# A four-layer graph network on one core: how the input tiles of the four projections are turned

## What is computed

```python
# layer 0: masked attention with 8 heads of 64
keys, queries, values = x @ Wks, x @ Wqs, x @ Wvs
x = layernorm(x + softmax(queries @ keys.T / 8 - 1e16 * (1 - adj)) @ values @ Wo)
# layer 1
x = layernorm(x + relu((adj @ x) @ W1.T + b1))
# layer 2
h, support = x @ edge_w, x @ weight
att = softmax(x @ node_w, axis=0) * softmax(where(adj > 0, h @ h.T, NEG_BIG), axis=1)
x = layernorm(x + (adj * att) @ support + b2)
# layer 3
x = layernorm(x + relu((a_norm @ x) @ W3.T + b3))      # a_norm: adj + I, scaled by degrees
```

## Time and profile before

| | us |
|---|---|
| median of 3 runs | 2541.1 (2539.39 to 2542.22) |
| profiled execution, its own time | 2541.41 |
| its span from first to last instruction | 2539.6 |
| PE busy | 2424.1, 95% of the span |
| DVE, ACT, POOL busy | 1545.9, 1364.0, 1148.7 |

### The profile page before, as it was taken

The page is one execution under the profiler, slowest core; times in us unless marked ns, Lnnn a source line. Parts: engine busy times, 40 slices in busy tenths (PEclk is TensorE's granted clock), DMA queues, the critical chain, the costliest instruction groups (busy, mean ns, idle before and its releaser), DMA issues. The chain is left out here.

```text
span 2539.6 us, 67049 instructions
## 1 busy us (share of the span) xinstructions
PE 2424.1 (95%) x24988; PEld 1557.7 (61%) x24988; DVE 1545.9 (61%) x3013; ACT 1364.0 (54%) x2036; POOL 1148.7 (45%) x971
## 2 busy tenths in 40 slices
PE   7997999999999999999879997999999999979998
PEld 6885777777777777777634443774444555534443
DVE  4435998898888898888632222555555566633222
ACT  3335888888888888888623221324434444323222
POOL 0005888888888888888601232001111113310323
PEclk9998999999999999999989999999999999989999
DMA  3216999999999999999743654215666779733664
GB/s 130 65 62 129 183 195 185 188 193 181 190 193 178 187 193 184 191 188 185 123 137 118 213 199 158 100 37 138 175 183 181 203 207 233 178 128 101 211 213 140
DMA packets 783644, 417.41 MB, mean 164 GB/s; under 512 B 691296, under 2 KB 717664, under 8 KB 774496
## 3 DMA queue, kind: packets, MB, share of 16 engines
q1 hardware_dynamic: 783456, 414.62, 70.7%
HBM read 203.55 MB, written 40.84 MB: 96 GB/s over the span
## 5 line engine op out<-in xcount | busy, mean ns | idle before, releaser
L806 DVE CUSTOM_DVE_ANT_0 att_scores<-att_slots,att_adj 128x1024 f32<-128x1024 f32 x528 | 575.7, 1091 | 41.6 <-POOL att_part_low L627 14.5
L627 POOL TENSOR_TENSOR att_part_low<-att_scores,att_part_high 128x1024 f16<-128x1024 f32 x352 | 574.8, 1651 | 12.0 <-ACT att_part_high L790 1.1
L751 ACT ACTIVATE att_scores<-att_scores,att_nmax 128x1024 f32<-128x1024 f32 x528 | 552.4, 1047 | 28.2 <-DVE att_lifted L817 26.0
L672 PE MATMUL att_slots<-l_kk,att_q 128*128 128x512 f16 x2112 | 466.5, 356 | 15.5 <-DMA att_q<-q_rows 8.9
L1345 PE MATMUL a_ps<-l_y,a_adj 128*128 128x512 f16 x1936 | 421.2, 381 | 9.0 <-DVE a_adj L1359 4.7
L825 DVE TENSOR_TENSOR att_near_low<-att_ps_t,att_near_high 128x512 f16<-128x512 f32 x528 | 316.4, 599 | 37.6 <-ACT att_near_high L760 35.9
L760 ACT ACTIVATE att_near_high<-att_ps_t 128x512 f16<-128x512 f32 x528 | 258.2, 524 | 150.0 <-PE att_ps_t L682 137.3
L1345 PEld LDWEIGHTS a_ps<-l_y,a_adj 128*128 128x128 f16 x1936 | 190.0, 98 | 240.1 <-DVE a_adj L1359 5.2
L672 PEld LDWEIGHTS att_slots<-l_kk,att_q 128*128 128x128 f16 x2112 | 195.2, 98 | 173.4 <-DVE att_least L806 24.9
L1090 PE MATMUL edge_ps_o<-l_sup,edge_pt_high 128*128 128x512 f16 x968 | 287.9, 379 | 1.7 <-DMA edge_pt_low<-edge_part_low 1.7
L1330 ACT ACTIVATE a_adj<-l_adj 128x2816 f16<-128x2816 f32 x44 | 112.0, 2549 | 291.1 <-DMA l_adj<-in_adj_cols 271.1
(11 more groups left out here) (152 smaller groups left out, 3863.2 us busy)
## 6 DMA issues: line engine op xcount, KB each, us to landing
l_adj<-in_adj_cols SPq DMA_DIRECT2D x44, 1408.0 KB, 6.1
l_adj_tiles<-in_adj SPq DMA_DIRECT2D x22, 1354.0 KB, 6.1
att_adj<-in_adj SPq DMA_DIRECT2D x66, 384.0 KB, 4.2
p_x_in<-x SPq DMA_DIRECT2D x66, 256.0 KB, 2.6
att_q<-q_rows SPq DMA_DIRECT2D x44, 256.0 KB, 3.8
a_xres<-x SPq DMA_DIRECT2D x44, 256.0 KB, 2.8
p_x_in<-in_x SPq DMA_DIRECT2D x22, 256.0 KB, 2.7
q_rows<-l0w_q_halves SPq DMA_DIRECT2D x22, 256.0 KB, 2.1
```

The lines of the kernel that those rows point to most:

```text
L627: nc.gpsimd.tensor_tensor(out=part[1][:, v, lo:lo + width], in0=sc[:, v, lo:lo + width], in1=part[0][:, v, lo:lo + width], op=ALU.subtract ...
L672: mm = nc.tensor.matmul(slots[:, slot, z:z + w], q[:, u, h % 2, a, h // 2, :], kk[:, h, lo + z:lo + z + w], start=a == 0, stop=a == 1)
L751: nc.scalar.activation(sc[:, v, lo:lo + width], sc[:, v, lo:lo + width], ACT.Exp, bias=nmax[:, v:v + 1], scale=-1.0).then_inc(exp_done, 1)
L806: nc.vector.tensor_tensor_reduce(out=sc[:, v, lo:lo + width], in0=slots[:, (NC * h + c) % 2, 0:width], in1=adj[:, u, lo:lo + width], scale ...
```

## The change

- p0 gets its input from the host in column form already (`x_cols`, the same number of bytes per tile, `columns=True`); there is nothing to turn, and the halves are made from `x_in`. Its loops stay as they are.
- p1, p2 and p3 read x in rows as before, but ACT and DVE split the rows first, from `x_in` in SBUF into a new f16 buffer `xr` of two tiles. Then SP issues two transposing transfers for each tile (one for each half, 128 x 512 f16, four blocks of 128 x 128), from `xr` to `xt`, which now holds four tiles. PE waits for both (`turned`, 32 for a tile).
- The PE transposes and their two PSUM banks are gone from all four projections.
- SP's order in p1 to p3: `late` is load(t), then the transposing transfers of tile t - 1. The load of tile 1 moves ahead of all but the first weight.
- In p1 to p3 the loops are written out (`each`).

```diff
-    def load(self, sp):
-        for (src, stage, _h, _l), loaded in zip(self.parts, self.loaded):
+    def load(self, sp, which=slice(None)):
+        for (src, stage, _h, _l), loaded in zip(self.parts[which], self.loaded[which]):
             sp.dma_start(stage, src).then_inc(loaded, 16)
...
+def each(eng, begin, end, step):
+
+
+    for t in range(begin, end):
+        step(t // 2, t % 2)
+
...
-        xt = s.sb("xt", [P, 2, 2, J, P], F16)
+        depth = 2 if columns else 4
+        xt = s.sb("xt", [P, depth, 2, J, P], F16)
+        xr = xt[:, :, :, :, :].rearrange("p u a j r -> p u a (j r)") if columns else s.sb("xr", [P, 2, 2, D], F16)
         junk = s.sb("junk", [P, D])
-        ps_t = s.ps("ps_t", [P, 2, BANK])
         ps_job = [s.ps(f"ps_job{n}", [P, 2, BANK]) for n in range(len(jobs))]
         x_loaded = [s.sem(f"x_loaded{u}") for u in range(2)]
-        turned = s.sem("turned")
         xt_high = s.sem("xt_high")
         xt_low = s.sem("xt_low")
+        turned = [s.sem(f"turned{u}") for u in range(2)]
...
+        over = pairs if columns else each
...
-                    sp.wait_ge(turned, 2 * m + u - 1)
+                    sp.wait_ge(xt_low, 2 * m + u - 1)
                     if score is not None:
                         sp.wait_ge(scored, 2 * m + u - 1)
-                sp.dma_start(x_in[:, u, :], x_rows[bass.ds((2 * m + u) * P, P), :]) \
-                    .then_inc(x_loaded[u], 16)
+                src = x_rows[bass.ds((2 * m + u), 1), :, :].rearrange("o p n -> (o p) n") if columns \
+                    else x_rows[bass.ds((2 * m + u) * P, P), :]
+                sp.dma_start(x_in[:, u, :], src).then_inc(x_loaded[u], 16)
...
+            def turn(m, u):
+
+                if not columns:
+                    t = 2 * m + u
+                    sp.wait_ge(xt_low, t + 1)
+                    if t >= depth:
+                        sp.wait_ge(made, nj * (t - depth + 1))
+                    for a in range(2):
+                        sp.dma_start_transpose(xt[:, t % depth, a, :, :], xr[:, u, a, :]).then_inc(turned[u], 16)
+
             def late(m, u):
                 load(m, u)
                 keep(*before(*before(m, u)))
+                turn(*before(m, u))
 
             load(0, 0)
-            own.load(sp)
+            own.load(sp, slice(0, 2))
             load(0, 1)
+            own.load(sp, slice(2, None))
             late_w.load(sp)
+            turn(0, 0)
             late(1, 0)
             late(1, 1)
             for dst, src in prefetch:
                 sp.dma_start(dst, src).then_inc(prefetched, 16)
-            pairs(sp, 4, T, late)
+            over(sp, 4, T, late)
+            turn(T // 2 - 1, 1)
...
-            def turn(m, u):
-                pe.wait_ge(x_loaded[u], 16 * m + 16)
-                if not (isinstance(m, int) and m == 0):
-                    pe.wait_ge(xt_low, 2 * m + u - 1)
-                for j in range(J):
-                    mm = nc.tensor.transpose(ps_t[:, u, j * P:(j + 1) * P],
-                                             x_in[:, u, j * P:(j + 1) * P], ident[:, :])
-                mm.then_inc(turned, 1)
-
             def multiply(m, u):
-                pe.wait_ge(xt_low, 2 * m + u + 1)
+                if columns:
+                    pe.wait_ge(xt_low, 2 * m + u + 1)
+                else:
+                    pe.wait_ge(turned[u], 32 * m + 32)
+                slot = u if columns else (2 * m + u) % depth
...
-            def step(m, u):
-                turn(*after(m, u))
-                multiply(m, u)
-
-            turn(0, 0)
-            step(0, 0)
-            step(0, 1)
-            pairs(pe, 2, T - 1, step)
+            multiply(0, 0)
+            multiply(0, 1)
+            over(pe, 2, T - 1, multiply)
             multiply(T // 2 - 1, 1)
...
             def split(m, u):
-                act.wait_ge(turned, 2 * m + u + 1)
+                act.wait_ge(x_loaded[u], 16 * m + 16)
                 if not (isinstance(m, int) and m == 0):
-                    act.wait_ge(made, nj * (2 * m + u - 1))
-                nc.scalar.activation(xt[:, u, 0, :, :], ps_t[:, u, :].rearrange("p (j r) -> p j r", j=J),
-                                     ACT.Copy, scale=X_S).then_inc(xt_high, 1)
+                    if columns:
+                        act.wait_ge(made, nj * (2 * m + u - 1))
+                    else:
+                        act.wait_ge(turned[u], 32 * m)
+                nc.scalar.activation(xr[:, u, 0, :], x_in[:, u, :], ACT.Copy, scale=X_S).then_inc(xt_high, 1)
...
+            over(act, 1, T - 1, step)
...
-                    out=xt[:, u, 1, :, :], in0=ps_t[:, u, :].rearrange("p (j r) -> p j r", j=J), scalar=X_S,
-                    in1=xt[:, u, 0, :, :], op0=ALU.mult, op1=ALU.subtract).then_inc(xt_low, 1)
+                    out=xr[:, u, 1, :], in0=x_in[:, u, :], scalar=X_S, in1=xr[:, u, 0, :], op0=ALU.mult,
+                    op1=ALU.subtract).then_inc(xt_low, 1)
...
+            over(dve, 1, T - 3, step)
...
-                project(nc, s, "p0", x, ident, [(wk, *key), (wv, *value), (wq, *query)],
+                project(nc, s, "p0", x_cols, ident, [(wk, *key), (wv, *value), (wq, *query)],
                         [("cols", *key, keys), ("rows", *value, values), ("cols", *query, queries)],
                         kept=(2, q_halves, q_rows), later=[(wo, *output)],
                         prefetch=[(row[:, :], vector.broadcast_to([P, D])) for row, vector in
-                                  ((b1_row, b1), (b2_row, b2), (b3_row, b3), (node_row, node_w))])
+                                  ((b1_row, b1), (b2_row, b2), (b3_row, b3), (node_row, node_w))], columns=True)
...
-        "x": padded(x, (NP, D)), "adj": padded(adj, (NP, N)), "adj_cols": cols,
+        "x": padded(x, (NP, D)), "x_cols": padded(x, (NP, D)).reshape(T, P, J, P).transpose(0, 3, 2, 1).reshape(T, P, D),
+        "adj": padded(adj, (NP, N)), "adj_cols": cols,
```

More of the change, by code:

```diff
@@ L149, in after @@
     return (m, 1) if u == 0 else (m + 1, 0)
+def each(eng, begin, end, step):
+    for t in range(begin, end):
+        step(t // 2, t % 2)
 def project(nc, layer, tag, x_rows, ident, weights, jobs, score=None, degrees=None, kept=None, later=(),
-            prefetch=()):
+            prefetch=(), columns=False):
     with ExitStack() as ctx:
@@ L265, in multiply @@
                     if kind == "rows":
-                        mm = product3(nc, ps_job[n][:, u, :], lambda a, j: xt[:, u, a, j, :],
+                        mm = product3(nc, ps_job[n][:, u, :], lambda a, j: xt[:, slot, a, j, :],
                                       lambda b, j: w[b][:, j, :])
@@ L271, in multiply @@
                                           lambda a, j: w[a][:, j, c * P:(c + 1) * P],
-                                          lambda b, j: xt[:, u, b, j, :])
+                                          lambda b, j: xt[:, slot, b, j, :])
                     mm.then_inc(made, 1)
-            def step(m, u):
-                turn(*after(m, u))
-                multiply(m, u)
-            turn(0, 0)
-            step(0, 0)
-            step(0, 1)
-            pairs(pe, 2, T - 1, step)
+            multiply(0, 0)
+            multiply(0, 1)
+            over(pe, 2, T - 1, multiply)
             multiply(T // 2 - 1, 1)
@@ L314, in _ @@
             step(0, 0)
-            pairs(act, 1, T - 1, step)
+            over(act, 1, T - 1, step)
             late_w.split_high(nc, act)
@@ L363, in _ @@
             step(0, 0)
-            pairs(dve, 1, T - 3, step)
+            over(dve, 1, T - 3, step)
             for t in range(T - 3, T - 1):
@@ L1386, in _, with build @@
                 step(T // 2 - 1, 1)
-def build(nc, x, adj, adj_cols, wk, wq, wv, wo, w1, b1, w2, b2, node_w, edge_w, w3, b3, out):
+def build(nc, x, x_cols, adj, adj_cols, wk, wq, wv, wo, w1, b1, w2, b2, node_w, edge_w, w3, b3, out):
     q_rows = nc.dram_tensor("q_rows", [NP, 2 * D], F16).ap()
```

## The result

| | before | after |
|---|---|---|
| median | 2541.31 us (2539.39 to 2542.22) | 2629.21 us (2626.23 to 2639.14) |
| profiled execution, its own time | 2541.41 | 2639.14, the slowest of the four |
| its span | 2539.6 | 2635.9 |
| mean granted clock | 0.982 | 0.965 |

What follows compares the result with a forecast made beforehand. The prediction took PE, busy 95% of the span, to bound the kernel before, with the transfers' path exposed after the change. It summed 2541.4 - 13 + 2 x 49.5 + 6 to 2633 us, range 2590 to 2665.

Steps and rivals of the forecast that it cites:

- p0, -13: In p0, no transposes and an earlier start of tile 0: 9 us and 4 us saved, together -13 us.
- The path, 6.1: In p1 to p3, from the end of tile t's products to the start of tile t + 2's: 6.1 us.
- The clock, +1.7 a pair: In p1 and p3, each pair's PE pause brings half clock once: 1.7 us a pair, 17 us a projection.
- The rival in which it stays up: In p1 and p3, PE's pauses become two short ones a pair and the clock holds: 2599 us, chance 0.27.
- p1, +49.5: p1, and p3 alike, gets longer by 26.5 (path) + 6 (prefetch) + 17 (clock) us.
- The prefetch, +6: In each of p1, p2, p3, transposing transfers queue behind two bulk transfers: PE waits 6 us once (bounds 3 and 9).
- p2, +6: In p2, a pair stays at 11.4 us, so only the prefetch stall adds: +6 us.
- Bandwidth is not the bound: A tile's 256 KB turned and 256 KB loaded take 2.1 us of DMA, so bandwidth does not bound.
- SP, 3.05 us a tile: In p1 to p3, SP issues a load and two transposing transfers in 3.05 us, under a tile's 4.35 or more.
- The last rival: Path stays under PE's work, at 2.6 us in p1 and p3, landing 0.4 us or less: 2499 us, chance 0.03.

Runs made afterwards that it cites:

- e1: The changed kernel with ACT and DVE writing the halves of tile t + 2 before the results of tile t in p1 to p3; 2557.77 us.
- e3: The changed kernel plus six unread matmuls of 512 columns behind each tile of p1 and p3, 264 in all; 2606.95 us.
- e2: The changed kernel with the prefetch of p1 to p3 cut into 16 pieces, one behind each of tiles 4 to 19; 2613.41 us.
- e5: The changed kernel with one transposing transfer of both halves of a tile (8 blocks) in place of two; 2582.97 us.
- e8: e7 with the prefetch cut into pieces as in e2; 2521.25 us.
- e9: e8 with four buffers for x and its halves, splits three tiles ahead, SP turning tile t, then loading tile t + 4; 2507.04 us.
- e6: e1 with SP's load of tile t directly ahead of the transposing transfers of tile t - 2, not behind them; 2556.84 us.
- e7: e6 with one transposing transfer per tile in place of two; 2543.24 us.

## Why the prediction was right

The forecast was 2633 (range 2590 to 2665), the median 2629.2, the profiled execution 2639.1. The mechanism was the forecast's: e1 shows that the order on ACT and DVE exposes the path, e3 that the half clock behind the pauses lengthens the pairs, e2 that the prefetch stalls. That the median came within 4 us is in part luck: the terms below are from the profiled execution, where the sum of the four stages was 94.9 us and the forecast's 92, with errors of -1.9 to +4.9 in the single ones. By its terms:

- **p0, -13:** -14.7. The first key product came at 10.79, as said, and the end of tile 0 moved from 25.00 to 21.57, by 3.4 us (4 taken): tile 0 took 10.8 us instead of 9.6, since its matmuls stood 0.11 us apart, half clock, until 16.7, for 5.9 us, where before they did so for 3.5. The 0.44 us a tile came as said. The load behind the prefetched rows, 1.9 us, had not been seen.
- **The path, 6.1:** 5.85, by the pair without the clock (8.44 - 2.59, where 8.7 was forecast). Mis-sized by a little in each piece: ACT and DVE took 1.92 us from ACT's start to the low half (before 1304.91 - 1302.86 = 2.05), SP 0.03 and 1.26 (0.1 and 1.3 taken), the landing 2.4 (2.5 taken). The pieces give 5.7; the rest of the 5.85 is that a tile's last matmul ends 2.75 us after its first one starts, and not 2.59.
- **The clock, +1.7 a pair:** +1.68, by e3. The rival in which it stays up came here for one pair of p1 only (1356.57 to 1364.99); e5 has it, at pauses of 1.9 us. The reason given for the tiles of a pair standing back to back, the stall at the beginning, is not borne out: in e2 they do so with a stall of less than half, and in the change they are back to back again from tile 17 on, with no stall ahead of it.
- **p1, +49.5:** +47.6. Up to the products of tile 5 the stage lost 15.0 us (1306.36 - 1264.90 = 41.5 after its first load, against 1303.00 + 3.03 - 1279.58 = 26.4 before), where two pairs and the stall were given 14.7; the eight pairs from there to tile 21 took 78.8 us instead of 48.0, 30.8 more (seven of them 9.8 to 10.1 us, one 8.4), and the last tile, in part at half clock, lost 1.7 (4.45 instead of 2.75). In p3 the pairs were a little longer, 82.8 us for the eight, and the stage lost 51.1.
- **The prefetch, +6:** the wait of tile 3 was 8.34, 5.3 over the pause that a pair has anyway. By e2 the prefetch as a whole cost 4.8 in p1, 7.9 in p2, 9.9 in p3.
- **p2, +6:** +10.9, the term most in error. Up to the products of tile 5 the stage lost 8.7 us (1664.75 - 1614.51 = 50.2 after its first load, against 1621.84 - 1580.32 = 41.5 before): the stall was 6.7 us, with one of 0.9 ahead of it; the granted clock was 0.63 over the 4.2 us behind it (window below), 1.6 us of work, for which the forecast had nothing; and the first product came 0.7 us later behind its load. Against these stand the transposes that are gone. The eight pairs behind, which the forecast took as even, took 93.0 us instead of 90.9: the short ones had 11.2 us (pauses of 0.5), others up to 12.5.

```profile
1652.00:1656.20 4.20, 4.05 (x48) 4.05 (x49) 1.59 (x3) 0.00 (x0) 0.00 (x0) 0.63 0.38 83
```

- **Bandwidth is not the bound:** right for the change (share 0.43), but it does not carry over to the mended kernels: e8 and e9 fill the DMA engines.
- **SP, 3.05 us a tile:** 3.2, since the load's issue behind transposing transfers takes 0.58 and not 0.33. It bounded nothing here, but it did in e6.
- **The last rival** has a wrong sum. A path of 2.6 us less 2.2 for ACT and DVE leaves 0.4 for SP's issues and the landing together, and the issues alone are 1.4 (0.1 + 1.3): in this order no landing time would have hidden the path under PE's work. What hid it, in e9, was another order and more buffers.

The rule of the Trainium skill on transposing transfers (Advanced Engine Details and Errata, X-Bar Transpose (TRN2)), that they are as fast as plain ones, would have made the landing 0.3 us shorter by the prediction (0.37 by the rates in the earlier trace rows); it was 2.4 to 2.5 us where 2.5 was taken, so no run here supports the shorter one.

## What to carry to other kernels

When work is moved from PE to transfers, count the whole path from the event that frees a buffer to the landing, and compare it with the work of PE that runs meanwhile; if an instruction order ties the start of that path to the tile before, mend the order first: here it was worth 71 of the 88 us, and with one transfer a tile, more buffers and a spread prefetch PE waited for almost none of them (e9). Cut a bulk transfer in pieces behind those that somebody waits for: that gave 16 us in e2 and 22 from e7 to e8. And price a pause of PE by the clock too: in the series of pauses of 3.1 us each cost 1.7 us more, in the series of 1.9 us none did, and single pauses of 2.4 to 2.9 us went either way.

## What the runs showed of the hardware

- Useless matmuls in the pauses made the kernel faster, 2629.2 to 2607.0: between them the clock stayed at 1.00 from pair to pair (e3).
- The issue of a transposing transfer holds SP for 1.24 to 1.25 us whether it turns four or eight blocks, so one of eight costs half of two of four. The one of eight lands after 2.8 us (median of e5), after 3.7 us in e8 where the DMA share is 1.04, and after up to 10.6 us behind a bulk prefetch (e5). There the issue itself can hold SP longer, 4.5 us in the change.
- A plain load issued directly behind a transposing transfer takes 0.58 us of SP (median of the 57 in the change), directly behind a plain one 0.43 to 0.47, and 0.33 where SP was free before it.
